# Middle tap folded into a weight tile, load and statistics taken among the first additions, and the group's tokens turned ahead of the fourth image's keys

## The reference, cut to what matters

```
t2  = conv 1x3 over channels (w2)
t3  = correlation of x, shifted by 2k columns, with x      (k = 0..6)
t9  = p9w * p6w * t3
t10 = sum over k of t9[k] * (t2 shifted by k - 3 rows)
t7  = conv 1x5 of t2, each channel on its own (w7)
t8  = conv 5x5 of x, dilation 2, each channel on its own (w8)
x   = x + t8 - (t10 - t7)
```

## Time and profile before

| | |
|---|---|
| median of 3 runs | 2685.22 us (2684.94 to 2689.61) |
| profiled execution | 2688.33 us, its span 2686.5 us |
| granted TensorE clock over the span | 0.93 |
| first stage | about 0 to 526 us; four steps with a convolution end near 130, 251, 367 and 479 us |
| TensorE, VectorE busy over the span | 89%, 87% |

### The profile page before, as it was taken

How to read it: one execution, slowest core, us unless ns; L and a number is a source line. 1 busy time by engine, 2 the same in 40 slices (tenths; PEclk the granted TensorE clock), 3 DMA queues, 4 the chain that set the end, 5 groups by cost and what they waited for, 6 DMA issues and landing times. The chain is left out here.

```text
span 2686.5 us, 46976 instructions
## 1 busy us (share of the span) xinstructions
PE 2400.2 (89%) x18454; PEld 969.8 (36%) x18454; DVE 2326.4 (87%) x4150; ACT 1593.8 (59%) x2090; POOL 408.4 (15%) x456
## 2 busy tenths in 40 slices
PE   3878888359999999999999999999999998889886
PEld 1443333112222222222222222222222223878785
DVE  4577877689999999999999999999999994899997
ACT  1243433427777777777777777777777777343333
POOL 0021211300000000100000000000000000465666
PEclk9989999659999999999999999999999999676777
DMA  7696784330202122022022021020220000232230
GB/s 171 164 251 194 215 246 141 140 81 1 61 1 61 47 81 61 13 49 61 1 61 61 1 61 45 17 61 10 52 61 1 25 25 37 85 109 98 84 109 25
DMA packets 68110, 206.29 MB, mean 77 GB/s; under 512 B 20630, under 2 KB 33554, under 8 KB 61234
## 3 DMA queue, kind: packets, MB, share of 16 engines
q1 hardware_dynamic: 64034, 185.27, 24.9%
q0 software_dynamic: 3040, 15.57, 1.6%
q10 hardware_dynamic: 816, 2.46, 0.3%
HBM read 80.14 MB, written 61.31 MB: 53 GB/s over the span
## 5 line engine op out<-in xcount | busy, mean ns | idle before, releaser
L1385 DVE TENSOR_REDUCE at_XM<-at_psX 128x1 f32<-128x448 f32 x2688 | 1546.3, 620 | 90.2 <-PE at_psX L1210 69.3
L1291 ACT ACTIVATE at_PR<-at_psS 128x896 f32<-128x896 f32 x1344 | 1163.7, 915 | 456.0 <-PE at_psS L1186 453.9
L1228 PE MATMUL at_psV<-at_PR,at_V 128*32 128x448 f32 x5376 | 645.0, 551 | 0.1
L1186 PE MATMUL at_psS<-at_US,at_KS 128*128 128x448 f16 x2688 | 636.5, 356 | 1.4 <-ACT at_PR L1291 0.7
L1210 PE MATMUL at_psX<-at_KS,at_US 64*128 64x448 f16 x1344 | 490.3, 365 | 64.4 <-DVE at_XM L1385 42.7
L1210 PE MATMUL at_psX<-at_KS,at_UH 64*128 64x448 f16 x1344 | 490.3, 365 | 0.0
L1210 PEld LDWEIGHTS at_psX<-at_KS,at_US 64*128 64x128 f16 x1344 | 124.6, 93 | 720.5 <-DVE at_XM L1385 661.3
L1186 PEld LDWEIGHTS at_psS<-at_US,at_KS 128*128 128x128 f16 x2688 | 201.4, 98 | 272.0 <-ACT at_PR L1291 111.6
L1348 POOL CAST at_mrow<-at_mt 7x128 f16<-7x128 f32 x64 | 18.0, 281 | 1611.2 <-DVE at_mt L1404 1258.4
L1703 POOL TENSOR_TENSOR fi_WE<-fi_WE 128x256 f32<-128x256 f32 (+1 forms) x224 | 214.6, 985 | 99.5 <-DVE fi_WE L1757 99.1
L415 PE MATMUL psA<-sb_stacks,sb_lhs 128*32 128x448 f32 x1568 | 157.4, 548 | 0.8 <-DVE sb_X L867 0.8
(11 more groups left out here) (217 smaller groups left out, 1987.9 us busy)
## 6 DMA issues: line engine op xcount, KB each, us to landing
sums<-at_O SPq DMA_DIRECT2D x16, 1568.0 KB, 6.3
fi_SUMS<-sums SPq DMA_DIRECT2D x16, 1568.0 KB, 6.7
sb_stacks<-sb_T SPq DMA_DIRECT2D x64, 270.5 KB, 7.4
sb_stacks<-sb_Xp SPq DMA_DIRECT2D x64, 248.8 KB, 10.3
sb_stacks<-sb_Xp SPq DMA_DIRECT2D x64, 248.0 KB, 5.8
sb_stacks<-sb_T SPq DMA_DIRECT2D x64, 172.5 KB, 11.5
at_KS<-key_stacks SPq DMA_DIRECT2D x32, 208.0 KB, 6.8
fi_RES<-residual SPq DMA_DIRECT2D x16, 400.0 KB, 7.2
```

The lines of the kernel that those rows point to most:

```text
L1186: last = nc.tensor.matmul(psS[:, at % 2, k, 0:TILE], KS[:, b, (2 * c + k) * P:(2 * c + k + 1) * P], US[:, b, t * TILE:(t + 1) * TILE], sta ...
L1228: last = nc.tensor.matmul(psV[C * q:C * q + C, 0:TILE], V[:, b, G * k + q, :], PR[:, (n * 2 * STEPS + 2 * q4 + q // 2) % PRS, q % 2, :], s ...
L1291: nc.scalar.activation(PR[:, f % PRS], psS[:, at % 2, :, 0:TILE], ACT.Exp).then_inc(p_ready, 1)
L1385: nc.vector.tensor_reduce(o, psX[:, (at + j) % 3, 0:TILE], AX.X, ALU.max).then_inc(x_done, 1)
```

## The change

`w7`'s middle tap (the tap without a shift) is no longer a pass of VectorE over 128x3136 elements. A 32x32 diagonal tile `w7d` is made once from it and added in `new_weights` to the block of `lhs10` for the unshifted row. `taps_row` runs for the taps 0, 1, 3 and 4, all ahead of `mixing`. SP therefore can issue `load(g + 1)` sooner, and does so ahead of the old group's second query store and third stores. VectorE takes four of the seven tiles' statistics (`sample`) ahead of the first addition, the other three after it, and normalises after the second. On TensorE `turn_output` goes ahead of the fourth image's keys and queries; ScalarE's order follows.

```diff
@@ sync, step
                 fill_stacks2(g, 1)
                 if old:
-                    store_stacks(m, 1, first[1])
-                    store_keys(m, 2, first[2])
+                    store_keys(m, 1, first[1])
                 if more:
                     sp.wait_ge(taps_done, g + 1)
                     for h in range(2):
                         sp.wait_ge(t2s_in[h], (g + 1) * STRIPS)
                     load(g + 1)
                 if old:
-                    store_queries(m, 2, first[2])
+                    store_queries(m, 1, first[1])
+                    store_stacks(m, 2, first[2])
@@ tensor, step
-                conv5(g, NT - 1, range(0, 4))
-                conv5(g, NT - 1, range(4, 7), keys_of(3))
+                conv5(g, NT - 1)
+                turn_output(g)
+                run(keys_of(3))
                 run(queries_of(3))
-                turn_output(g)
@@ scalar, step
-                    keys(m, 2, first[2])
-                    query_high(m, 2, range(QSETS), first[2])
                 if more:
                     act.wait_ge(stat_var, g + 2)
                     nc.scalar.activation(rs[:], var[:], ACT.Sqrt).then_inc(stat_std, 1)
                 if old:
+                    keys(m, 2, first[2])
+                    query_high(m, 2, range(QSETS), first[2])
                     squares(m, 3, first[3])
                     deviations(m, 3)
                     high_parts(m, 3, first[3])
-                    keys(m, 3, first[3])
-                    query_high(m, 3, range(QSETS), first[3])
                     act.wait_ge(res_out, m * G * 16 + G * 16)
...
                 if old:
+                    keys(m, 3, first[3])
+                    query_high(m, 3, range(QSETS), first[3])
                     act.wait_ge(ks_out, m * G * 16 + G * 16)
                     act.wait_ge(us_out, m * G * 16 + G * 16)
@@ vector
+            nc.vector.tensor_scalar(w7d[:], eye4[0:C], w7e[0:C, 2:3], None, ALU.mult)
...
-            def statistics(g):
+            def sample(g, tiles):
                 dve.wait_ge(x_in, g * 16 + 16)
-                for i in range(NT):
-                    last = nc.vector.bn_stats(stats[:, i, :], XI[:, i * TILE:(i + 1) * TILE])
-                link(last)
+                for i in tiles:
+                    mark(nc.vector.bn_stats(stats[:, i, :], XI[:, i * TILE:(i + 1) * TILE]))
+
+            def statistics(g, tiles=range(NT)):
+                sample(g, tiles)
+                settled()
...
-                last.then_inc(lhs10_ready, 1)
+                            if s == 0 and i == 0:
+                                mark(last)
+                settled()
+                nc.vector.tensor_tensor(lhs10[0:C, 0], lhs10[0:C, 0], w7d[:].unsqueeze(1).broadcast_to([C, G, C]),
+                                        ALU.add).then_inc(lhs10_ready, 1)
@@ vector, step
-                taps_row((0,))
-                if old:
+                if old:
+                    taps_row((0,))
                     scale(m, 1, z)
                     taps_row((1,))
                     low_parts(m, 1, z)
-                    taps_row((2,))
+                    taps_row((3, 4))
+                else:
+                    taps_row((0, 1, 3, 4))
                 mixing(g)
...
                     scale(m, 2, z)
-                else:
-                    taps_row((1, 2))
+                if more:
+                    sample(g + 1, range(0, 4))
+                if old:
+                    low_parts(m, 2, z)
+                dve.wait_ge(taps_done, g + 1)
                 add((0,))
-                if old:
-                    low_parts(m, 2, z)
+                if more:
+                    statistics(g + 1, range(4, NT))
                 add((1,))
-                taps_row((3, 4))
-                dve.wait_ge(taps_done, g + 1)
+                if more:
+                    normalise(g + 1)
                 add((2,))
                 if old:
                     query_low(m, 2, z)
                 add((3,))
-                if more:
-                    statistics(g + 1)
                 if old:
                     z = first[3]
                     centre(m, 3, z)
-                if more:
-                    normalise(g + 1)
                 add((4,))
```

More of the change, by code:

```diff
@@ L42 @@
 GR = 2 * XW
-ORDER_0, ORDER = 14, 46
+ORDER_0, ORDER = 20, 52
 class Ahead(NamedTuple):
@@ L170, in prepare @@
         w7e = sb("w7e", [P, 5])
+        w7d = sb("w7d", [C, C])
         p6 = sb("p6", [P, 2])
@@ L932, in step @@
                     scale(m, 2, z)
-                else:
-                    taps_row((1, 2))
-                add((0,))
+                if more:
+                    sample(g + 1, range(0, 4))
                 if old:
                     low_parts(m, 2, z)
+                dve.wait_ge(taps_done, g + 1)
+                add((0,))
+                if more:
+                    statistics(g + 1, range(4, NT))
                 add((1,))
-                taps_row((3, 4))
-                dve.wait_ge(taps_done, g + 1)
+                if more:
+                    normalise(g + 1)
                 add((2,))
```

## The result

| | before | after |
|---|---|---|
| median of 7 runs | 2688.32 us | 2698.52 us (2695.04 to 2701.65) |
| ratio | | 1.0041, 95% interval 1.0026 to 1.0056 |
| profiled execution, its span | 2688.33, 2686.5 us | 2695.93, 2694.1 us |
| stage 2 begins (ScalarE's table load) | 526.41 us | 534.13 us |

Slower by 0.41%, some 11 us, where 2686.6 was predicted (1.4 us above the median of 2685.2 then known) and 2691.5 was the end of the range. The stage of the change ends 7.7 us later and the span is 7.6 us longer; the profiled execution is near the low end of its seven.

The account below looks back on a forecast made before the run. No engine was full: TensorE set the time inside output tiles, and the chain changed hands at step boundaries. Terms -2.0, +0.6, -0.4 and +3.2 gave +1.4 us on 2685.2, so 2686.6; range 2680 to 2691.5.

Parts of the forecast that it names:

- Load and statistics: Steps 1 and 2: load lands some 5 us early; first addition 1.4 us later, TensorE loses about 0.45 us.
- rival (c): GpSimd's residual addition contends with VectorE's statistics: +3.4 us on the sum, 2690; chance 0.07.
- The end: Stage end, no strips wanted: turning, keys, queries and last low part delay VectorE's last token work; 3.2 us lost.
- +0.6 into step 2: Boundary into step 2: fourth tile's wait for the strips' second half, landing late, costs 0.6 us.
- -0.4 into step 3: Boundary into step 3: strips' second half at 390.9 against 391.33 before, 0.4 us won.
- What TensorE lost, the earlier strips and the 8.53 us wait of VectorE pay back.: Step 1: step 0's 7.1 us TensorE stall at the load is made up, 2.0 us won.
- So the first copy is at 358.3: Boundaries: ScalarE's first copy of turned tiles waits 6.95 us after the residual store's command; 356.6 would be possible.
- Rival (a): Residual store lands in some 4 us, turning starts 1.7 us earlier at two boundaries: sum -4.3, 2681; chance 0.14.
- (b): Boundaries: strips' second half needs 24.6 us, not 21.2; low clock could slow keys too; sum +5.9, 2691; chance 0.15.
- the late end: Boundaries: strips' second half lands 21.2 us after issue plus 1.2 for the query store, at 390.9; taken for the forecast.
- hole of some 8 us: Boundaries: DMA queues carry nothing between the strips' first half landing and the second half's issue, some 8 us.
- takes the place of the wait removed: Boundaries: image 3's last low part holds VectorE's next step until 368.2, was 366.74.

Follow-up runs that it names:

- e3: Changed kernel, but in step 0 alone VectorE does the first two additions ahead of all statistics; ratio 1.0008, 2689.1 us.
- e5: Changed kernel with the fourth image's keys and queries ahead of the turning again and step 0's first two additions ahead of all statistics; 0.9923, 2665.5 us.
- e6: Kernel before with only the turn order changed: turning ahead of the fourth image's keys and queries; ratio 1.0059, 2702.2 us.
- e4: Kernel before with only the middle tap folded into lhs10, one VectorE pass less per step; ratio 0.9994, 2686.1 us.
- e8: Changed kernel with the first half of the Xp strips issued after the seventh output tile instead of the fourth; ratio 1.0122, 2719.7 us.
- e1: Changed kernel with the turn order undone: fourth image's keys and queries ahead of the turning again; ratio 0.9957, 2674.0 us.
- e10: Changed kernel with the fourth image's keys, not its queries, ahead of the turning again; ratio 1.0011, 2691.3 us.
- e9: Changed kernel with both strip halves issued in one run and the fourth image's key and query stores from ScalarE's queue; ratio 1.0049, 2699.9 us.

## Why the prediction was wrong

**The runs as a sum.** The change splits in the same way on two bases. With step 0 as in the change, the turn order costs 22.6 us (1.0041 against 0.9957); without step 0's stall 22.8 (e3, 1.0008 against e5, 0.9923). The stall costs 8.9 and 9.1. What is left, load and statistics among the additions of steps 1 and 2 with the tap folded and SP's and ScalarE's orders to match, gives 20.7 (e5 against before). -20.7 + 22.7 + 9.0 = +11.0, the measured 0.41%. The two losses add; the gain and the order do not: with the order in place the same rest is worth 13.7 (e3, 1.0008, against e6, 1.0059), and the order alone costs the kernel before 15.9. So of the 22.7 some 16 are a loss against before and some 7 a gain withheld. The rest was not split further. The forecast of +1.4 was added up by place and not by piece, and no term of it says what the order costs against the change without it.

**What held.** The middle tap: nothing on the kernel before (e4; not shown for the changed one), and the diagonal took 0.28 us (predicted under 0.3). Load and statistics: the load landed before it was needed in steps 1 and 2; the first addition came later and TensorE lost 0.49 and 0.53 us (0.45 predicted). Contention, rival (c), didn't happen: GpSimd's addition took 1.90 us beside the statistics. The Trainium skill's GPSIMD Engine Reference, Specifications, names contention with VectorE instructions in a two-port mode or with two SBUF inputs, and statistics have one; the trace agrees, with 1.90 beside them and 5.06 us beside a two-input pass (step 1, at 150.42 us). In step 0 TensorE stood 6.46 us (7.1 predicted), VectorE started step 1 at 137.08 (136.0), and the strips took 21.3 us from idle queues (21.2). The end: +3.01 against +3.2, by the chain that was named: last low part at 486.7, token work at 487.21.

**The steps that failed.** The terms of the sum that failed are those of the two boundaries: +0.6 into step 2 measured +4.65, and -0.4 into step 3 measured +2.04; step 1 and the end held. Points (2) to (5) say where the difference arose, and (1) what was wrong behind a term that came out right.

(1) "What TensorE lost, the earlier strips and the 8.53 us wait of VectorE pay back." As a forecast against before its -2.0 was right at the mixing (-1.98), though not by the path named: `scale` came 0.9 us earlier and not 2.0. But it closed the account too soon. The same rearrangement without the stall would have given 8.7 us there (e3: 183.81). VectorE's 8.53 us wait of before went away with the earlier strips; behind it VectorE itself became the bound of step 1, so the late start counts in full.

(2) "So the first copy is at 358.3", with 6.95 us from the residual store's command to the copy. Into step 3 it held: 6.81 us. Into step 2 it was 8.99 (command's end 232.99, copy 241.98). The flights from issue to landing are 7.5 and 6.6 us in the kernel before, 9.5 and 7.3 in the changed one. The first half of its strips goes out 11.6 us ahead of the store instead of 6.2, but that is so at both boundaries, and why one flight took 9.5 and the next 7.3 the runs don't settle. Rival (a), with its 4 us, is refuted: beside the strips it is never under 6.5, and 2.7 without them (e8). The Trainium skill, DMA: Bandwidth & Descriptors, Queues, rings and completion order, has the engines alternate between queue rows packet by packet; the runs don't contradict that, but the half of the engines' time that I read into it is not what a store gets here.

(3) The turning was counted at 4.0 us from the first copy: 4.7 less 0.7. It took 5.5 (241.98 to 247.5); in e1, where TensorE stood only 1.18 us, 4.3. TensorE came out of its stand at its lower clock level (17 transposes in 4.20 us, and 0.58 in the window; 0.50 from 364 to 366 us at the next boundary, behind a stand of 2.06). That the clock is what made the turning longer fits these rows and was not tested by itself. The clock was named under (b) and then not priced. Keys and queries were 0.7 us shorter than reckoned. With (2), VectorE's first pass came 1.6 us past the forecast into step 2 (store +2.0, its command 1.3 sooner, turning less keys +0.9) and 1.3 into step 3 (+0.3 and +1.0).

(4) Strips, second half: from VectorE's first pass to TensorE's fourth tile 23.5 us at both boundaries, where 22.7 was the late end. So they landed some 23.1 us after the first issue. Rival (b) named this, with 24.6 us and a sum of +5.9; its place was right, and the fourth tile does wait for strips (1.95 and 2.16 us). The "hole of some 8 us" is about 11 at the first boundary (242 to 253, with the key store alone in it).

(5) Not counted at all: the transfers behind those strips are late too. ScalarE's square waits 5.46 us for a key store, where it waited 4.32 before (the line below), and from the fourth tile to the mixing step 2 takes 35.60 us where it took 34.01. These terms are the miss in the profiled executions, where the forecast was +1.4 and the stage ends 7.7 us later: into step 2, 1.6 + 0.8 + 1.6 = 4.0 of the 4.05 us; into step 3, 1.3 + 0.8 + 0.35 = 2.45 of 2.44. The spans then differ by 7.6 us. The medians differ by some 3 us more; that lies in the spread of the changed kernel's runs, and no trace shows where it arises.

```profile
289.69 0.87 ACT L553 ACTIVATE sb_KS<-sb_XH 128x800 f32<-128x800 f32 x1 [4.32 <-DMA key_stacks<-sb_KS]
```

The deeper fault is in how I summed. I asked of each boundary what it does against before, and found that the new order "takes the place of the wait removed". The place was right, and it hid that all the rest was worth 20 us, which the order gave back whole. What made the old order good can be seen in the earlier trace rows and the TensorE rows beside them: the residual store takes 7 us, and keys and queries are the work that fills them. e1's rows show that filling intact with the store landing nearly as late as in the changed kernel (9.0 us after its issue, where it was 9.5).

**What stays open.** Which share of the order's 22.6 us is idle time of TensorE, which the clock and which the transfers was not separated; e8 puts 3.3 us of mixing to first pass on the store at one boundary, e10 some 8 us of the whole on the keys. Holding image 3's last low part behind VectorE's first pass, which would free that pass, wasn't tried. Nor was the middle tap left on VectorE in the changed kernel.

## What to carry to other kernels

Before work is moved ahead of other work on an in-order engine, look for what the moved work waits for and what has been filling that wait: here a store's 7 to 9 us of flight were filled by the very keys and queries that were put behind it. Put a piece that was worth nothing on the old kernel back on the new one before calling it worthless, as what was idle time there may be gone. Price each part of a joint change against the version without that part, too, and not only against the kernel before; a small sum can be a gain of 20 us and two losses that eat it. Where, as in step 0, the load arrives late, an addition that frees the bottleneck engine's next tile goes ahead of the work that waits for it (9 us here).

## What the runs showed of the hardware that was not expected

A store of 400 KB landed 2.7 us after its issue in quiet queues (e8). Beside the strips it took 6.5 (e6) to 9.5 us (changed kernel) on GpSimd's queue, and stores of 416 KB on ScalarE's took 8.3 and 10.2 (e9). TensorE's granted clock fell inside a stand of 4.24 us; it was 0.58 over the 6 us from 242, which is mostly the 1.2 GHz level, with TensorE busy for 5.08 of them, and 1.00 in the 6 us that followed.
